# Attention with four-slot probability rings, weighing three pieces behind, later evictions, and a quarter of the low parts on GpSimd

## The reference, cut to what matters

```python
qkv = x @ W_qkv                                    # x is normalised; 16 heads of 64
q, k = (apply_rope(q), apply_rope(k))
dots = jnp.einsum('bhid,bhjd->bhij', q, k) * scale
dots = jnp.where(causal, neg, dots)
attn = jax.nn.softmax(dots, axis=-1)
out = jnp.einsum('bhij,bhjd->bhid', attn, v)
out = out.transpose(0, 2, 1, 3).reshape(b, n, INNER)
out = jax.nn.relu(out @ W_o1) @ W_o2               # then a layer norm
```

## Time and profile before

| what | value |
|---|---|
| median of 3 runs | 5959.87 us (5954.83 to 5964.68) |
| profiled execution, its own time | 5942.21 us |
| its span | 5940.3 us |
| granted TensorE clock, mean of the span | 0.798 |
| TensorE busy | 3936.9 us (66%) |
| VectorE busy | 4405.1 us (74%) |
| ScalarE busy | 2385.7 us (40%) |
| GpSimd busy | 2650.9 us (45%) |

### The profile page before, as it was taken

The page is one execution under the profiler, slowest core; times in us unless marked ns, Lnnn a source line. Parts: engine busy times, 40 slices in busy tenths (PEclk is TensorE's granted clock), DMA queues, the critical chain, the costliest instruction groups (busy, mean ns, idle before and its releaser), DMA issues. The chain is left out here.

```text
span 5940.3 us, 81715 instructions
## 1 busy us (share of the span) xinstructions
PE 3936.9 (66%) x27691; PEld 2390.1 (40%) x27691; DVE 4405.1 (74%) x5229; ACT 2385.7 (40%) x3604; POOL 2650.9 (45%) x1626
## 2 busy tenths in 40 slices
PE   3976555444444545489495388888855888888395
PEld 2652111111111111156385155555633555556384
DVE  6873799999999999988301578888866888887301
ACT  1223432333333333212221166667743666667231
POOL 0211676676676776512202056655303646650202
PEclk9998655566666555599598599999977999999597
DMA  2000000000000000000254222222102212220254
GB/s 73 0 4 6 0 0 0 0 0 0 0 0 0 0 0 0 15 0 0 87 170 127 73 46 54 54 46 46 35 29 55 54 43 51 53 52 6 89 183 136
DMA packets 216325, 235.76 MB, mean 40 GB/s; under 512 B 61547, under 2 KB 181284, under 8 KB 214880
## 3 DMA queue, kind: packets, MB, share of 16 engines
q1 hardware_dynamic: 206304, 207.35, 13.1%
q0 software_dynamic: 8704, 24.35, 1.2%
q10 hardware_dynamic: 1024, 0.13, 0.0%
HBM read 116.95 MB, written 31.59 MB: 25 GB/s over the span
## 5 line engine op out<-in xcount | busy, mean ns | idle before, releaser
L971 PE MATMUL mix_scan_y<-mix_scan_hc,ident 128*128 128x512 f32 x512 | 476.9, 1086 | 957.1 <-DVE mix_scan_hc L904 957.1
L2040 DVE TENSOR_TENSOR att_b_prob_low<-att_b_prob,att_b_prob_high 128x1024 f16<-128x1024 f32 (+2 forms) x640 | 780.8, 1220 | 237.3 <-ACT att_b_prob_high L2002 223.7
L895 DVE TENSOR_TENSOR_SCAN mix_scan_h<-mix_scan_a_bar,mix_scan_state,mix_scan_dub 128x512 f32<-128x512 f32 x256 | 834.1, 3297 | 0.1
L2067 DVE TENSOR_REDUCE att_b_neg_max<-att_b_peek 128x1 f32<-128x1024 f32 (+7 forms) x768 | 684.3, 905 | 75.5 <-PE att_b_peek L1897 39.1
L2008 ACT ACTIVATE att_b_prob<-att_b_score,att_soft 128x1024 f32<-128x1024 f32 (+2 forms) x640 | 631.9, 987 | 169.6 <-PE att_b_score L1917 102.7
L852 ACT ACTIVATE mix_scan_a_bar<-mix_val,mix_A 128x512 f32 (+1 forms) x256 | 170.8, 714 | 1219.4 <-DVE mix_scan_h L895 1219.4
L971 PEld LDWEIGHTS mix_scan_y<-mix_scan_hc,ident 128*128 128x128 f32 x512 | 149.9, 323 | 1233.8 <-DVE mix_scan_hc L904 1102.0
L2002 ACT CAST att_b_prob_high<-att_b_prob 128x1024 f16<-128x1024 f32 (+2 forms) x640 | 587.9, 919 | 30.4 <-PE att_b_o L1945 13.1
L1941 PE MATMUL att_b_o<-att_b_vh,att_b_prob_high 128*128 128x65 f16 x4352 | 465.4, 195 | 179.4 <-DVE att_b_heads L2058 88.6
L1941 PEld LDWEIGHTS att_b_o<-att_b_vh,att_b_prob_high 128*128 128x128 f16 x4352 | 400.6, 98 | 306.3 <-DVE att_b_prob_low L2040 205.9
L816 POOL TENSOR_TENSOR mix_scan_dub<-mix_u,mix_scan_b_row 128x512 f32<-128x512 f32 x128 | 279.7, 2185 | 412.8 <-ACT mix_scan_b_row L856 412.8
(11 more groups left out here) (329 smaller groups left out, 9595.6 us busy)
## 6 DMA issues: line engine op xcount, KB each, us to landing
moe_w<-in_L_ffn_W_dram SPq DMA_DIRECT2D x64, 1024.0 KB, 8.1
att_b_crossed<-att_b_raw SPq DMA_DIRECT2D x512, 64.0 KB, 2.0
att_b_q_both<-att_b_halves SPq DMA_DIRECT2D x256, 64.0 KB, 2.0
att_b_k_twice<-att_b_halves SPq DMA_DIRECT2D x256, 64.0 KB, 2.0
moe_slots_in<-moe_route_zero SPq DMA_DIRECT2D x2, 4096.0 KB, 14.2
moe_exp_x<-moe_slots_in SPq DMA_DIRECT2D x32, 256.0 KB, 4.2
moe_slots_out<-moe_exp_y POOLq DMA_DIRECT2D x32, 256.0 KB, 6.5
att_b_k_low<-att_b_halves SPq DMA_DIRECT2D x128, 64.0 KB, 2.0
```

Of the source, the lines that this page charges most:

```text
L895: dve.tensor_tensor_scan(cols(hs, 0, m), cols(a_bar, b, m), cols(dub, b, m), state[:, at:at + 1], ALU.mult, ALU.add).then_inc(scanned, 1)
L971: done = pe.matmul(y_ps[m][:, :], ident[:, :], cols(hc, n % 2, m), start=(n == 0), stop=(n == S_N - 1))
L2040: dve.tensor_tensor(prob_low[:, at:at + width], prob[:, at:at + width], prob_high[:, at:at + width], ALU.subtract).then_inc(low_ready, 1)
L2067: last = dve.tensor_reduce(neg_max[:, first + col:first + col + 1], peek_ps[:, base:base + nb * P], AX.X, ALU.max, negate=True)
```

## The change

- `prob_high` and `prob_low` get four slots (`RING`), `prob` keeps two. `weigh` and `take` come three steps behind (`BEHIND`) instead of two, and the waits for free slots are counted for four.
- ScalarE and VectorE do a side job's eviction one step later, between the high or low part and the exponentials or `take`, except in the lead-in turn.
- GpSimd computes the low parts of pieces 25, 27, ..., 39 (`LOW_ON_POOL`), behind its rotations and ahead of `split_weights`. They have a semaphore of their own, and `wait_low` chooses the right one for TensorE and ScalarE.
- In the lead-in turn the stacks are issued by ScalarE, in front of its copies and behind the last one, and the last "qk" job moves from step 17 to step 15.
- `wo` and `headsT` get one buffer instead of two. The load of `wo` moves from the start of the turn on SyncE to behind stack 4 (in `LAST`, behind `spread_queries`).

```diff
+BEHIND = 3
+LOW_ON_POOL = range(25, STEPS, 2)
+RING = 4
...
 def side_job(kind, v):
-    if v not in SIDE or not has_pair(kind, SIDE[v][2]):
+    jobs = {15 if kind == BEFORE and u == 17 else u: job for u, job in SIDE.items() if has_pair(kind, job[2])}
+    if v not in jobs:
         return None
...
+        def wait_low(eng, t, m):
+            if isinstance(t, int) and t * STEPS + m < 0:
+                return
+            t, m = (t, m) if m >= 0 else (t - 1, m + STEPS)
+            on_pool = sum(u in LOW_ON_POOL for u in range(m + 1))
+            if m in LOW_ON_POOL:
+                eng.wait_ge(low_ready_pool, t * len(LOW_ON_POOL) + on_pool)
+            else:
+                eng.wait_ge(low_ready, t * (STEPS - len(LOW_ON_POOL)) + m + 1 - on_pool)
+
+        def low_part(eng, t, m, ready):
+            at, to = m % 2 * SPAN, m % RING * SPAN
...
+            if eng is nc.gpsimd:
+                wait_apart(eng, high_ready, piece(t, m + 1), (masks, MASKS))
+            else:
+                eng.wait_ge(high_ready, piece(t, m + 1))
+                wait_unless_first(eng, p_done, piece(t, m + 1 - RING))
+            eng.tensor_tensor(prob_low[:, to:to + width], prob[:, at:at + width], prob_high[:, to:to + width],
+                              ALU.subtract).then_inc(ready, 1)
...
         # SyncE
                 if has_pair(kind, 0):
-                    load_out_weights(t, b)
                     spread_queries(t, b, 1)
+                if kind == LAST:
+                    load_out_weights(t)
...
-                        stack(t, b, i, kind)
+                        if kind != BEFORE:
+                            stack(sp, t, b, i, kind)
+                        if i == 4 and has_pair(kind, 0):
+                            load_out_weights(t)
...
         # GpSimd
                 if kind in (FIRST, MIDDLE, LATE):
                     for i in range(QK_JOBS):
                         rotate(pool, cr, t, i, kind)
+                if has_pair(kind, 0):
+                    for m in LOW_ON_POOL:
+                        low_part(pool, t, m, low_ready_pool)
                 if kind in (BEFORE, FIRST, MIDDLE):
                     split_weights(t + 2)
...
         # TensorE
-                    if v >= 2 and has_piece(kind, v - 2) or v < 2 and has_piece(kind, -1):
-                        weigh(t, b, v - 2)
+                    if has_piece(kind, v - BEHIND):
+                        weigh(t, b, v - BEHIND)
...
         # ScalarE
                     if has_piece(kind, v - 1):
                         high_part(t, v - 1)
+                    job = side_job(kind, v if kind == BEFORE else v - 1)
+                    if job:
+                        if kind == BEFORE and job[0][0] == "qk" and job[0][1] >= 2:
+                            stack(act, t, b, job[0][1] - 2, kind)
+                        side(t, b, *job[0])
+                        if kind == BEFORE and job[0] == ("qk", QK_JOBS - 1, 1):
+                            for i in (QK_JOBS - 2, QK_JOBS - 1):
+                                stack(act, t, b, i, kind)
                     if has_piece(kind, v):
                         exponents(t, v)
...
-                wait_unless_first(act, low_ready, piece(t, m - 1))
+                wait_low(act, t, m - 2)
...
         # VectorE
-                    if has_piece(kind, v - 1):
-                        low_part(t, v - 1)
-                    if v >= 2 and has_piece(kind, v - 2) or v < 2 and has_piece(kind, -1):
-                        take(t, b, v - 2)
+                    if has_piece(kind, v - 1) and (v - 1) % STEPS not in LOW_ON_POOL:
+                        low_part(dve, t, v - 1, low_ready)
+                    job = side_job(kind, v if kind == BEFORE else v - 1)
+                    if job:
+                        side(t, b, kind, *job[0])
+                    if has_piece(kind, v - BEHIND):
+                        take(t, b, v - BEHIND)
```

More of the change, by code:

```diff
@@ L1581, in side_job @@
 def side_job(kind, v):
-    if v not in SIDE or not has_pair(kind, SIDE[v][2]):
+    jobs = {15 if kind == BEFORE and u == 17 else u: job for u, job in SIDE.items() if has_pair(kind, job[2])}
+    if v not in jobs:
         return None
-    earlier = [SIDE[u] for u in sorted(SIDE) if u < v and has_pair(kind, SIDE[u][2])]
+    earlier = [jobs[u] for u in sorted(jobs) if u < v]
     before = {BEFORE: None, FIRST: ("mrow", 0, 0)}.get(kind, ("out", 5, -1))
-    return SIDE[v], ([before] + earlier)[-1]
+    return jobs[v], ([before] + earlier)[-1]
 def in_turns(eng, turn):
@@ L1686, in rotate, with stack @@
             assert c.n == ROPE_STEPS
+        def stack(eng, t, b, i, kind):
+            r = i % 2
+            at = (1 - b) * SEQ + i // 2 * GRP
+            to = slice(at, at + GRP)
+            ready, through = qk_count(t + 1, i + 1), piece(t, 0)
+            if i == 0 and not isinstance(t, int):
+                ready, through = eng.to_reg(ready), eng.to_reg(through)
+            eng.wait_ge(roped, ready)
+            if i == 0 and kind in (MIDDLE, LATE):
+                eng.wait_ge(scored, through)
+            for h in range(2):
+                mine = slice(h * HEAD, (h + 1) * HEAD)
+                if r == 0:
+                    eng.dma_start(q_both[h][0:HEAD, to], high(r)[mine, :]).then_inc(stacked[r], 16)
+                    eng.dma_start(q_both[h][HEAD:P, to], low16(r)[mine, :]).then_inc(stacked[r], 16)
+                else:
+                    eng.dma_start(k_twice[h][0:HEAD, to], high(r)[mine, :]).then_inc(stacked[r], 16)
+                    eng.dma_start(k_twice[h][HEAD:P, to], high(r)[mine, :]).then_inc(stacked[r], 16)
+                    eng.dma_start(k_low[h][0:HEAD, to], low16(r)[mine, :]).then_inc(stacked[r], 16)
         @block.sync
@@ L1737, in cross @@
                         .then_inc(crossed_over[i % 2], 16)
-            def stack(t, b, i, kind):
-                r = i % 2
-                at = (1 - b) * SEQ + i // 2 * GRP
-                to = slice(at, at + GRP)
-                ready, through = qk_count(t + 1, i + 1), piece(t, 0)
-                if i == 0 and not isinstance(t, int):
-                    ready, through = sp.to_reg(ready), sp.to_reg(through)
-                sp.wait_ge(roped, ready)
-                if i == 0 and kind in (MIDDLE, LATE):
-                    sp.wait_ge(scored, through)
-                for h in range(2):
-                    mine = slice(h * HEAD, (h + 1) * HEAD)
-                    if r == 0:
-                        sp.dma_start(q_both[h][0:HEAD, to], high(r)[mine, :]).then_inc(stacked[r], 16)
-                        sp.dma_start(q_both[h][HEAD:P, to], low16(r)[mine, :]).then_inc(stacked[r], 16)
-                    else:
-                        sp.dma_start(k_twice[h][0:HEAD, to], high(r)[mine, :]).then_inc(stacked[r], 16)
-                        sp.dma_start(k_twice[h][HEAD:P, to], high(r)[mine, :]).then_inc(stacked[r], 16)
-                        sp.dma_start(k_low[h][0:HEAD, to], low16(r)[mine, :]).then_inc(stacked[r], 16)
             in_turns(sp, turn)
@@ L1989, in side @@
                     act.wait_ge(h_turned, turn_count(p, i + 1))
-                    act.wait_ge(o_ready, out_count(p, 2 * (i - 1) if i >= 2 else 0))
-                    act.copy(headsT[:, i % 2 * GRP:(i % 2 + 1) * GRP], side_ps[:, :]).then_inc(hT_ready, 1)
+                    act.wait_ge(o_ready, out_count(p, 2 * i))
+                    act.copy(headsT[:, :], side_ps[:, :]).then_inc(hT_ready, 1)
             def width_of(m):
@@ L1998, in high_part @@
             def high_part(t, m):
-                at, width = m % 2 * SPAN, width_of(m)
+                at, to, width = m % 2 * SPAN, m % RING * SPAN, width_of(m)
                 act.wait_ge(expd, piece(t, m + 1))
-                wait_unless_first(act, p_done, piece(t, m - 1))
-                act.copy(prob_high[:, at:at + width], prob[:, at:at + width]).then_inc(high_ready, 1)
+                wait_unless_first(act, p_done, piece(t, m + 1 - RING))
+                act.copy(prob_high[:, to:to + width], prob[:, at:at + width]).then_inc(high_ready, 1)
             def exponents(t, m):
```

43 lines of the change are left out of this document (15 added, 28 removed).

## The result

The changed kernel takes 6077.6 us, the median of 4 runs (6061.4 to 6086.8), against 5960.7 for the kernel before on the same chip. The ratio is 1.019, with a 95% interval of 1.017 to 1.022: slower, by 117 us where 26 were forecast, and above the forecast's range of 5942 to 6022. GpSimd's share of the low parts is eight of forty, a fifth and not a quarter.

A forecast was written before the change was run, and what follows sets the result against it. No engine was full overall; GpSimd's rotations bound steps 0 to 17, VectorE steps 18 to 39. -62 - 2 + 97 - 4 - 3 = +26 us, from the median 5959.9 to 5986 us, range 5942 to 6022.

The forecast's parts named there:

- The weight split behind the low parts: Start of turns 1 to 6: the first projection waits 6.9 us for GpSimd's late split, 8.1 with slow clock; +97 us.
- Steps 0 to 17: First stage of a turn: GpSimd's rotations still set the pace, the exponentials start earlier; gain 0.8 us, bounds 0 and 2.
- Steps 18 to 24: Middle stage of a turn, VectorE's: it starts less in arrears; gain 1.6 us, bounds 0 and 2.5.
- Steps 25 to 39: Last stage of a turn: eight low parts leave VectorE, TensorE limits next; gain 2.0 us, bounds 0 and 3.2.
- Together 4.4 us in each of the fourteen turns: Gains of the three stages summed over the fourteen turns with a successor: -62 us.
- if the last stage doesn't shrink: Sign that the forecast is wrong; steps 25 to 39 were expected to take about 35.7 us.
- The lead-in: Turn before the eight: stacks go to ScalarE, last job moves from slot 17 to 15; -1.5 us per batch, -3.
- The last turn: Last turn of each batch: no projections, paced by ScalarE; an estimated -1 us each, -2.
- The loop jump, -4: Once a batch TensorE loses 3.58 us at the loop's jump; most passes inside the new wait for the split: -4 us.
- At nothing: One `wo` buffer and one `headsT` counted as costing nothing; 0.7 us a turn if the first cover failed.
- The decoupling: Rival 1, steps 18 to 39: gains 7.4 us a turn, more than the late split costs; -39, 5921 us; chance 0.16.
- Exclusion: Rival 2: GpSimd and VectorE hold the port pair exclusively, so steps 25 to 39 gain nothing; +54, 6014 us; chance 0.13.

The follow-up runs named there:

- shorter rotations: The kernel before with GpSimd's multiplication by the sine cut to 32 of 512 columns outside the lead-in, result left incomplete: 5908.7 us, 0.9926.
- rings-alone version: The changed kernel with evictions in their own step and no low parts on GpSimd, weighing three behind kept: 5974.3 us, 1.0033 against the kernel before.
- early evictions: The changed kernel with evictions at the end of their own step again, the weight split still late: 6018.2 us, 1.0103 against the kernel before.
- the split between: The changed kernel with evictions in their own step and the weight split in two pieces, behind GpSimd's low parts 25 and 31: 5947.4 us, 0.9995.
- rings two behind: The changed kernel with evictions in their own step, no low parts on GpSimd and weighing two steps behind: 5948.3 us, 0.9995 against the kernel before.

## Why the prediction was wrong

The direction was right, and the largest term held, its place as well as its price within an eighth. What failed is the gain set against it: -62 us, which was not there. The forecast was short by 91 us (117 measured, 26 said). The pairs of runs put the loss in two places: 64 us for the late split (1.0103 to 0.9995) and 54 for the late evictions (1.0194 to 1.0103); with both undone, the rings, three behind and GpSimd's low parts are at the time of the kernel before (0.9995), where the sum of the forecast without the split has them some 67 us below it (-62 - 2 - 3).

- *"The weight split behind the low parts ... +97"* held. The wait was 6.0 to 6.2 us in ten of the twelve turns (6.9 said), and the stage grew by 7.05 on average with the half clock behind it (8.1 said): +84.6 measured in the traces. Taking it out brought 70 us with late evictions (1.0194 to 1.0077) and 64 with early ones (1.0103 to 0.9995). The split itself took 2.7, 2.3 and 1.6 us: VectorE was idle beside it.
- *"Steps 0 to 17 ... taken 0.8"* held in kind: 0.42. The eighth copy starts 0.09 us behind the sixth rotation's end in all 14 turns before and in 10 of 14 after, and shorter rotations gave 3.4 us a turn.
- *"Steps 18 to 24 ... taken 1.6"* held: 1.8. The late evictions bring it (20.70 to 18.66 by themselves).
- *"Steps 25 to 39 ... taken 2.0"* failed, and with it *"Together 4.4 us in each of the fourteen turns"*, -62: this is the step that made the forecast wrong. The stage grew by 1.9 us, which was one of the prediction's own signs of being wrong ("if the last stage doesn't shrink"). The fourteen turns, without the first stretch of the twelve, gave 4.4 us in sum (-5.0 - 21.7 + 22.3 + 1.9 - 1.9) where 62 were said. The prediction saw that an "out" job's eviction would stand behind a low part and be waited for in steps 27 and 31; it priced that at part of the gap to 3.2 us and let VectorE's freed 7.3 us decide. In the runs that freed time was worth nothing while the evictions were late (1.0077 against 1.0072), and 23 us, 1.6 a turn, once they were not. The lower bound of 0 was wrong: what the evictions and three behind put in front of TensorE cost more than the freed time gave.
- Weighing three behind was counted as a gain alone. Alone it costs 23 us. The idle time before `weigh` did fall by more than half, as forecast (179 to 53), but the wait moved on to the peeks and to the jobs in `side_ps`. It also brings a chunk's end one step nearer to the turning job in steps 25, 29 and 35; moving those jobs away won back nothing that can be told.
- *"The lead-in ... -3"* came out +17.7. The crossing chain got shorter as thought (117.0 us on average with evictions in their own step, 118.9 before). The later evictions' part was not followed into the lead-in: the description says "except in the lead-in turn", yet the code's new place ahead of the maximum holds there too. It costs 10 to 11 us a batch.
- *"The last turn ... -1 each"* came out +5.8 each. Chunk ends and evictions again, with no late split: 3.3 us of it stay in the rings-alone version's steps 25 to 39 and none with two behind.
- *The loop jump, -4*: held. In turn 3, behind the jump, TensorE's wait for the split is 2.52 us in the first batch and 3.68 in the second, against 6.0 to 6.2 in the other ten: 6 us less.
- *At nothing* (`wo`, `headsT`): right, within 0.1%.

Of the rivals, none was it. The decoupling paid less, not more. Exclusion came nearest in time (6014), but it isn't the cause: the hold is real, but in steps 25 to 39 of the changed kernel only one of VectorE's five low parts of 1024 columns in a turn meets one of GpSimd's, for 0.15 us as a rule, and the same low parts gain 23 us where nothing else stands in the way. What the prediction said against that rival held. The late evictions were no rival at all, though they cost 54 us.

In the traces the clock went with the waits: in turns 0 to 6 of both batches the granted clock stood at 0.50 for 51 us before, 201 after, 170 with early evictions, 85 with the split between, 65 with rings two behind. Part of every wait's price is this; no run tells that part apart.

No version that computes the whole result beats the kernel before by more than can be told: the best two, at 0.9995, are at its time. The one run below it is the one with shorter rotations, which leaves a part of them out.

## What to carry to other kernels

When an instruction is moved within one engine's order, write down what now stands in front of it and who waits for it, in every kind of turn the code has, not only in the one that was profiled; a lead-in has other neighbours. Idle time in front of one instruction is not time to be won: here it moved to the next instructions that wait (108 us off `weigh`, 142 onto `peek`). So add up an engine's idle time over all its instructions before and after, not that of the one at which the change aims. An engine's hole is a place for work only up to the point where its own late producer (here the split) is due; put the producer between the new pieces, not behind them, and look at what the other engine does at that moment.

## What the runs showed of the hardware

VectorE's low part and a two-input instruction of GpSimd don't overlap. In the traces of the kernel before, of the changed one and of the version with the split between, a low part of 1024 columns that starts while GpSimd is in a two-input subtraction, multiplication or addition takes what is left of that instruction plus 1.08 us. That holds within 0.01 us in all 368 cases with more than 0.15 us left; by itself the low part takes 1.22. For `wl` at 4123.97 above that is 1.38 + 1.08 = 2.46. This is where the 1585 ns of the earlier trace rows come from: they are the mean of low parts of 1.20 to 2.07 us. VectorE's maximum of 1024 columns, which reads PSUM, stayed at 1.22 us beside GpSimd's low parts. The rule of exclusion that the prediction weighed is borne out for this pair of instructions, and what it costs depends on how often the two meet.

TensorE lost the clock after short waits too. In the rings-alone version two waits of 1.26 and 0.99 us, with a few matmuls of a peek and of scores between them, came ahead of a granted clock of 0.50; ten of its fourteen turns have such a fall around step 25, of 3.4 us each, against one with two behind and none in the kernel before. With two behind one wait of 1.36 and two of 0.16 and 0.23 us at the same place left it at 1.00. First rings alone, then two behind:

```profile
4122.64 0.23 PE L1932 MATMUL att_b_peek<-att_b_k_twice,att_b_q_both 128*128 128x128 f16 x1 [1.26 <-DVE att_b_neg_max L2098]
...
4125.00:4126.00 1.00, 1.00 (x20) 0.94 (x18) 1.00 (x1) 0.00 (x0) 1.00 (x1) 0.50 0.72 148
```

```profile
4105.12 0.19 PE L1976 MATMUL att_b_o<-att_b_vh,att_b_prob_high 128*128 128x65 f16 x1 [1.36 <-DVE att_b_heads L2089]
...
4107.30 0.20 PE L1976 MATMUL att_b_o<-att_b_vh,att_b_prob_high 128*128 128x65 f16 x1 [0.23 <-DVE att_b_prob_low L1690]
```

GpSimd's low part of 1024 columns took 2.13 us beside a busy VectorE, within 0.1 of the estimate from its 768-column subtraction, while VectorE's own stayed at 1222 ns in that stage of turn 5. The changed kernel's runs spread over 25 us, those of the kernel before over 10.
